# Five banks, an earlier shift, later copies, filler matmuls and four buffers for differences at the border between projections and attention

## What is computed

```python
q = (x @ wq); k = (x @ wk); v = (x @ wv)          # 16, 4 and 4 heads of 16
q = q * cos + rotate_half(q) * sin                # k likewise
scores = einsum('bqkgd,bskd->bkgqs', qg, k) / 4
attn = softmax(scores)                            # over 1024 keys
x = layernorm(x + einsum('bkgqs,bskd->bqkgd', attn, v) @ wo)
h = silu(x @ Wg.T) * (x @ Wu.T)                   # Wg = (gate_w - 128) * gate_scale
x = layernorm(x + h @ Wd.T)
```

## Time and profile before

| | us |
|---|---|
| three plain runs | 902.16, 904.97, 907.14 |
| their median | 904.97 |
| profiled execution, its own time | 901.66 |
| span of the profile | 899.8 |
| TensorE busy | 880.8 |
| VectorE busy | 742.7 |
| ScalarE busy | 713.4 |
| POOL busy | 268.5 |

### The profile page before, as it was taken

One profiled execution on the slowest core, in us unless ns is written; L12 is line 12 of the kernel. 1 busy time (PEld: TensorE's weight loads), 2 busy tenths in 40 slices (PEclk: granted clock), 3 DMA queues, 4 the chain that ended last, 5 costly groups with the idle time before them and its releaser, 6 DMA issues.

```text
span 899.8 us, 16217 instructions
## 1 busy us (share of the span) xinstructions
PE 880.8 (98%) x5658; PEld 459.5 (51%) x5658; DVE 742.7 (83%) x1655; ACT 713.4 (79%) x929; POOL 268.5 (30%) x232
## 2 busy tenths in 40 slices
PE   8999999999999999999999999999999999999996
PEld 3334444444444444444444444444436888888885
DVE  5578999999999999999999999999955455665545
ACT  1467999999999999999999999999985565555564
POOL 6763340035434000001001000220104765665555
PEclk9997999999999999999999999999999999999999
DMA  7993543323353132232214313131111010110001
GB/s 245 292 242 97 122 123 85 88 84 76 93 120 70 45 77 58 56 77 68 52 48 91 73 46 78 44 62 36 39 54 52 30 48 24 48 47 25 24 24 48
DMA packets 53458, 69.98 MB, mean 78 GB/s; under 512 B 17344, under 2 KB 26560, under 8 KB 53376
## 3 DMA queue, kind: packets, MB, share of 16 engines
q1 hardware_dynamic: 50280, 65.53, 28.8%
q0 software_dynamic: 864, 3.15, 1.3%
q10 hardware_dynamic: 2232, 0.25, 0.2%
HBM read 46.74 MB, written 16.25 MB: 70 GB/s over the span
## 4 chain that ended last, share of the span: by engine, by line
PE 84%; DVE 5%; DMA 3%; ACT 2%; issue 2%; POOL 1%; SPq 1%; ACTq 0%; POOLq 0%; DVEq 0%
PE pv_bank L1367 25%; PE ring_bank L1279 23%; PE pair_bank L1425 13%; PE pair_bank L1488 12%; PE pv_bank L1514 3%; PE ring_bank L1514 3%; DVE block_max L846 3%; PE ring_bank L1377 2%; DMA q_sb<-shift 1%; ACT probs L1180 1%; PE pair_bank L1313 1%; DMA q_parts<-low 1%; DMA sinq_sb<-sin_q 1%; POOL rotated L588 1%; PE ring_bank L1392 1%
## 5 line engine op out<-in xcount | busy, mean ns | idle before, releaser
L1180 ACT ACTIVATE probs<-pair_bank 128x1024 f32<-128x1024 f32 x512 | 495.8, 1023 | 43.6 <-PE pair_bank L1425 43.4
L846 DVE TENSOR_REDUCE block_max<-ring_bank 128x1 f32<-128x384 f32 x854 | 486.2, 608 | 16.9 <-PE ring_bank L1279 7.2
L1279 PE MATMUL ring_bank<-k_max,q_sb 48*128 48x512 f32 x1126 | 313.4, 443 | 1.8 <-DVE block_max L842 0.5
L1279 PEld LDWEIGHTS ring_bank<-k_max,q_sb 48*128 48x128 f32 x1126 | 151.1, 185 | 267.0 <-DVE block_max L846 116.5
L1367 PE MATMUL pv_bank<-probs,v_all 128*17 128x512 f32 x2048 | 270.5, 600 | 0.7 <-ACT probs L1180 0.7
L1425 PE MATMUL pair_bank<-q_sb,k_sb 50*128 50x512 f32 x1024 | 221.8, 428 | 2.5 <-DMA q_sb<-shift 1.7
L1037 DVE SCALAR_TENSOR_TENSOR hid<-pair_bank,up_s,silu 128x512 f32<-128x512 f32 x63 | 47.1, 747 | 85.1 <-ACT silu L1236 85.1
L1425 PEld LDWEIGHTS pair_bank<-q_sb,k_sb 50*128 50x128 f32 x1024 | 99.4, 186 | 30.7 <-ACT probs L1180 9.2
L755 POOL TENSOR_TENSOR hid_l<-hid,hid_h 128x512 fp32r<-128x512 f32 x63 | 81.7, 1297 | 86.3 <-ACT hid_h L1215 85.6
L670 POOL TENSOR_TENSOR attn<-attn,inv_rows 128x1024 f32<-128x1024 f32 x7 | 16.7, 2390 | 301.7 <-DMA inv_rows<-inv_d 228.6
L842 DVE CUSTOM_DVE_ANT_0 above<-ring_bank,above 128x512 f32<-128x512 f32 x136 | 93.2, 687 | 5.8 <-PE pair_bank L1279 3.9
(11 more groups left out here) (142 smaller groups left out, 862.9 us busy)
## 6 DMA issues: line engine op xcount, KB each, us to landing
k_max<-k_parts SPq DMA_DIRECT2D x96, 96.0 KB, 3.7
q_sb<-q_parts SPq DMA_DIRECT2D x64, 128.0 KB, 3.5
k_sb<-k_parts SPq DMA_DIRECT2D x96, 64.0 KB, 2.3
attn<-xT SPq DMA_DIRECT2D x8, 512.0 KB, 6.0
q_parts<-high SPq DMA_DIRECT2D x16, 256.0 KB, 3.7
q_parts<-low SPq DMA_DIRECT2D x16, 256.0 KB, 4.3
q_sb<-q_parts SPq DMA_DIRECT2D x64, 64.0 KB, 3.7
attn<-pv_sb SPq DMA_DIRECT2D x128, 32.0 KB
```

The costliest lines, as they stand in the source:

```text
L846: dve.reduce_max(block_max[half % 2][:, col:col + 1], bank[:, 0:width], axis=AX.X).then_inc(ring_used, 1)
L1180: act.activation(probs[t % 2][:, 2 * pr:2 * pr + 2, :], pair_bank[pr][:], ACT.Exp, scale=D ** -0.5).then_inc(probs_ready, 1)
L1279: pe.matmul(bank[:, 0:last - first], q_sb[k][rows, i, qt * P:(qt + 1) * P], k_max[k // QH][rows, kind * CH + first:kind * CH + last], star ...
```

## The change

- The entries after `wide_from` go round five banks instead of six; the second half of `pair_bank[0]` is left out.
- Early differences go round four buffers: the two `above` and two slices of `probs[1]`, which the loop writes in its step 1 for the first time; there ScalarE gets a wait for the last early reader.
- SP issues `load_shift(0, 0)` ahead of both stores of the last block. POOL waits for the end of the turn ahead of its `low_of(7, 0)`.
- ScalarE's two last copies move into its share of the last list: values after the second entry, keys after the sixth.
- TensorE gets a filler (`keep_busy`, an fp32 matmul of 128 rows, 128 x 128, whose result is not used) ahead of 12 of the 13 entries of the last list, and ahead of each of the five entries of loop step 0, which now all come ahead of the scores.

```diff
+VALUES_COPIED = 1
+KEYS_COPIED = 5
+WIDE_BANKS = 5
...
-            turn = (pos - wide_from) % (2 * BANKS)
-            return BANKS + turn if turn < BANKS else (wide_from + turn) % BANKS
+            turn = (pos - wide_from) % WIDE_BANKS
+            return (2 * BANKS - 1, BANKS)[turn] if turn < 2 else (wide_from + turn - 2) % BANKS
...
+        early_aboves = readers[:early_entries].count("above")
+        early_above = [above[0][:], above[1][:], probs[1][:, 0, :], probs[1][:, 1, :]]
+        def above_of(count):
+            return early_above[(count - 1) % 4] if count <= early_aboves else early_above[(count - 1) % 2]
+        def above_free(count):
+            return count - 4 if count <= early_aboves else count - 2
...
+                    if last and c == 1:
+                        load_shift(0, 0)
                     store_q(m, 0)
...
-                    if last and c == 1:
-                        load_shift(0, 0)
                     store_q(m, 1)
...
+                if m == BLOCKS - 1 and j == 0:
+                    after_turn(0)
                 pool.wait_ge(hi_ready, 2 * m + j + 1)
...
-                    buf = above[(count - 1) % 2]
+                    buf = above_of(count)
...
-                        if count > 2:
-                            act.wait_ge(*last_reader[count - 2])
-                        act.activation(above[(count - 1) % 2][:], bank_of(key), ACT.Relu).then_inc(above_ready, 1)
+                        if above_free(count) > 0:
+                            act.wait_ge(*last_reader[above_free(count)])
+                        act.activation(above_of(count), bank_of(key), ACT.Relu).then_inc(above_ready, 1)
...
+                    if n == BLOCKS and at == VALUES_COPIED:
+                        copy_v_rows(B - 1)
+                    if n == BLOCKS and at == KEYS_COPIED:
+                        copy_k_rows(B - 1)
...
-            copy_k_rows(B - 1)
-            copy_v_rows(B - 1)
...
+                            if g == 1 and pr == 0:
+                                act.wait_ge(*last_reader[early_aboves])
...
+            def keep_busy(bank):
+                pe.matmul(bank, wq_sb[:, 0, 0:P], x_in[BLOCKS - 1][:, 0, 0:P], start=True, stop=True)
             def early_work(n, h):
-                for key in early[n, h]:
+                for at, key in enumerate(early[n, h]):
+                    if n == BLOCKS and at:
+                        keep_busy(pair_bank[0][:, 1, 0:P])
...
-                                for index in ((BANKS, BANKS + 1), (BANKS + 2, BANKS - 1))[pr]:
+                                for index in ((BANKS,), (BANKS + 2, BANKS - 1))[pr]:
...
-                        if t in MIXED:
+                        if first and k == 0 and t == 0:
+                            for i in range(len(entries)):
+                                keep_busy(pv_bank[:, 0:P])
+                                maxima(i)
+                            scores(0)
+                            scores(1)
+                        elif t in MIXED:
```

More of the change, by code:

```diff
@@ L582, in _, with after_turn @@
             pool.wait_ge(memsets, 6)
+            def after_turn(half):
+                pool.wait_ge(shift_ready, half + 1)
             def rotate(m, j):
@@ L661, in _ @@
             pool.wait_ge(v_used, 2 * B)
-            def after_turn(half):
-                pool.wait_ge(shift_ready, half + 1)
             def normalize(p):
@@ L840, in take_max @@
                     dve.wait_ge(sem_above, count)
-                    buf = above[(count - 1) % 2]
-                    dve.tensor_tensor_reduce(out=buf[:], in0=bank, in1=buf[:], scale=1.0, scalar=-3.0e38, op0=ALU.add, op1=ALU.max,
+                    buf = above_of(count)
+                    dve.tensor_tensor_reduce(out=buf, in0=bank, in1=buf, scale=1.0, scalar=-3.0e38, op0=ALU.add, op1=ALU.max,
                                              accum_out=block_max[half % 2][:, col:col + 1]).then_inc(ring_used, 1)
```

## The result

The changed kernel takes 916.38 us at the median of six runs (914.16 to 920.9), the kernel before 903.41 (900.05 to 907.14). The ratio is 1.0156 with a 95% interval of 1.0127 to 1.0185: slower, outside the stated range.

The account below looks back on a forecast made before the run. PE was taken to bound the kernel; 17 filler rounds put the first scores at 79.1 us, plus 5.9 makes 85.0 against 80.58, +4.4, so 906.1, plus 1.6 offset 907.7 us. Range: 900.5 to 912.5, likeliest case 905 to 910.

Parts of the forecast that it names:

- The bound and the place: PE bounds the kernel, busy 880.8 of 899.8 us; time is to be won only where projections give way to attention.
- the border: Where projections end and the attention loop begins: PE waits, then the clock falls to 1.2 GHz from 70 to 80 us.
- the anchor: Start of the products of loop step 1, 80.58 us before the change; its shift goes one to one into the end.
- Early turn, copies, buffers, banks: Before the loop: turn 1.1 us earlier, difference cycle 1.55 to 1.22 us, banks cost 0; gains lost behind the fillers.
- the sum: First scores at 79.1 us plus 5.9 gives 85.0 against 80.58: +4.4 us, 906.1 in the profile's terms.
- The filler's round: Last list and loop step 0: each of 17 fillers adds a round of 0.82 us, 13.9 us in all.
- the rival in which weights load under columns: At the fillers: a round of 0.43 us, 1.6 us faster, 901.7 us with the offset; chance 22%.
- the one with one of two changes hidden: At the fillers: one change of rows costs nothing, a round of 0.64 us, +1.4 us, 904.7 with the offset; chance 10%.
- The clock: From the last list through loop step 0: the sum priced work at full clock, with 2.4 us won back.
- the way from the first scores to the anchor: Loop steps 0 and 1: 3.3 + 1.0 + 1.6 = 5.9 us, against 8.35 us before at half clock.
- a rival of 18%: Clock falls all the same near the loop's start: ten microseconds at 1.2 GHz lose 5 us, 912.7 with the offset; 18%.
- The offset of the runs: Plain runs' median lies 3.3 us above the profiled execution; half, 1.6 us, was added, with 0 and 3.3 as bounds.

Follow-up runs that it names:

- e4: Kernel before with the early turn alone (POOL waits for the turn, shift writes go ahead of both stores): 903.17 us, ratio 0.9999.
- e5: Changed kernel without fillers and with two buffers for the early differences instead of four: 902.86 us, ratio 0.9996.
- e12: Changed kernel with each filler replaced by one rounded 48-row matmul of 512 columns, and two buffers for early differences instead of four: 902.26 us, ratio 0.9985.
- e3: Changed kernel with each filler replaced by two rounded 48-row matmuls of 512 columns: 903.77 us, ratio 1.0009.
- e6: Changed kernel with the 12 fillers of the last list and none in loop step 0: 913.17 us, ratio 1.0093.
- e2: Changed kernel with fillers of 512 columns instead of 128, same rows and places: 918.42 us, ratio 1.0165.
- e7: Changed kernel with each filler replaced by one rounded 48-row matmul of 512 columns: 902.26 us, ratio 0.9966.
- e1: Changed kernel without its 17 fillers, all else kept: 903.11 us, ratio 1.0003.
- e8: Changed kernel with two 48-row, 512-column fillers ahead of 12 list entries, none in step 0, step 0 in the order before the change: 903.36 us, ratio 1.0005.
- e9: Changed kernel with one 48-row, 512-column matmul per filler, plus five more ahead of the scores of step 1: 901.84 us, ratio 0.9982.
- e11: Changed kernel with one 48-row, 512-column filler ahead of 12 list entries, none in step 0, step 0 in the old order: 900.95 us, ratio 0.9967.

## Why the prediction was wrong, point by point

**The bound and the place** were right. All that changed, but for the 0.76 us ahead of the border, lies between 65 and 95 us, and it goes one to one into the end: the anchor moves by 14.6 us, the span by 14.4.

**Early turn, copies, buffers, banks: right, as far as the changed kernel shows them.** The turn's cast takes 0.17 us, the pair after it starts 65.84 - 65.04 = 0.80 us after the border's first block instead of 66.16 - 64.28 = 1.88, the 1.1 us of the sum. VectorE's waits are for PE alone, so the gain is lost, as the sum said. e4 adds what I had seen only in part: without the later copies the turn's gain stops at ScalarE. What four buffers gain by themselves no run could tell from nothing (e5, e12).

**The filler's round: right.** 0.82 was worked out from a projection's round and the transposes; 0.84 us was measured in the four whole rounds before the clock fell, and 1.48 us with 512 columns. So the rival in which weights load under columns is refuted here, and so is the one with one of two changes hidden (0.64). The Trainium skill ("TensorE: Matmul & The Clock Gate", Part 2, Step-by-step) has the queue pull a weight load ahead where the row groups don't conflict or the load goes to the background buffer. Here, after a 128-row matmul, it didn't: the load at 66.60 starts 0.42 us after the filler's own, when the columns are through. No run shows which of the two conditions was missing.

**The clock: wrong.** The sum priced all seventeen rounds at 0.82 us and the way from the first scores to the anchor at 5.9 us, both at 2.4 GHz, and counted 2.4 us as won back by the clock; that the clock holds was the premise under both terms. The fall was a rival of 18%, and its price was 5 us, for a stretch as long as today's. This premise is the step that failed, and in the rival the length of the stretch. The clock fell in the fifth round, at 69.98 us, and was down for 23.9 us. The rounds behind it took 1.45 us where they have a full block, instead of 0.84; by the start of the first scores that is 87.07 - 79.1 - 0.76 = 7.2 us in all. The way from the first scores to the anchor took 95.16 - 87.07 = 8.1 instead of 5.9 us. Together 9.4 us: 85.0 + 0.76 + 9.4 = 95.2, the anchor that was measured. Where the clock held, the way was 82.82 - 76.72 = 6.1 us (e3), so the 5.9 was sound by itself.

I had looked for the danger behind the first scores and had written only in passing that in a round 0.43 of 0.82 us are columns. e6 shows the fall inside the list, and e2 that four times the columns in the same places keep the clock at 1.00 there. That is as far as the cause is shown. The number of columns does not decide alone: the clock also fell in the profiles of e7 and e12, whose fillers have 512 columns.

**The offset of the runs.** I added 1.6 us, half the distance between profile and median. The median of the changed kernel is 916.38, its profiled execution 916.1, so the distance was 0.3 us there; for the kernel before, with six executions, it is 903.41 - 901.66 = 1.75. This error of 1.3 us doesn't matter beside the clock's.

**Signs.** The forecast was no change, with slower at 30%. The sum's 906.1 with the clock's 9.4 and the 0.76 from ahead of the border is 916.3; the profiled execution took 916.1. The rival as priced gave 912.7, which also lies outside my range of 900.5 to 912.5: the right mechanism with half its cost, at 18%.

## What to carry to other kernels

Don't take it as given that filler matmuls hold the clock: in the profile PE was busy 5.00 of 5 us with fillers of 128 columns and the clock fell, and stayed down for 23.9 us, against 10.2 with the idle gaps that they had replaced. With 512 columns in the same places it held through all of them. Before adding fillers, price the case in which the clock falls with them in place, for then each filler costs its round at 1.2 GHz.

Price a filler by a round read between the same neighbours; this part of the sum held to 0.02 us. Here fillers with the rows of their neighbours, 512 columns and one record (rounded instead of fp32) were the cheaper ones, two of them in a round of 0.57 us. With one such filler an entry the kernel was 0.3% faster than the one before, with two it was level, and with none and the old order of step 0 it was 0.2% faster, so a gain of the fillers themselves is likely at most.

When a gain lies ahead of a stretch at the lower clock, look at what comes out behind it: in e1 PE was busy 8.8 of the 10 us from 65 to 75 instead of 8.2, and the time did not change.

## What the runs showed of the hardware

The spread of the kernel before from run to run goes with the clock. Over the 91 executions beside the experiments the correlation between the mean granted clock and the time is -0.92: at 0.984 it takes 906.9 to 908.9 us, at 0.992 it takes 900.6 to 903.1. A difference of 0.01 in the mean goes with 8.3 us. By that, 10.2 us at 1.2 GHz, which lower the mean by 0.0057, cost 4.7 us, close to the 5.1 us of work that PE loses in them.

A change between 48-row and 128-row matmuls costs 0.2 us each way at 2.4 GHz: of a round of 0.84 us, 0.43 are columns (0.22 and 0.21) and the other 0.41 are weights that load under no columns (rows of PEld above). That makes an estimate of 17 x 0.41 = 7 us in the changed kernel, before the lower clock adds to it.

The clock also falls at other places in some executions: in e2 and e3 for 3.4 us at 41.4 and 40.3 us, after PE waited 2.62 and 2.27 us for the first keys (it did not fall there in the profiles before and after, with waits of 0.69 and 1.41 us), and in e2 for 3.4 us at 96.0, behind the first scores, after waits of 0.81 and 0.42 us. That was the place I had feared.

What decides whether the clock falls at this border with matched fillers (it did in the profiles of e7, e8, e9, e11 and e12, not in that of e3), and how long a stretch at 1.2 GHz lasts (3.4, 10.2, 13.7, 20.5, 23.9 and 30.7 us were seen here), was not settled.
